# A four-layer graph network on one core: layer 0's edge loop with the expanded rows added on TensorE, the next expansion ahead of the sums, and the weights' store on ScalarE's queue

## What is computed

```python
xl = (x @ W_l + b_l).reshape(n, HEADS, C)
xr = (x @ W_r + b_r).reshape(n, HEADS, C)
e = (edge_attr @ W_e).reshape(-1, HEADS, C)
g = leaky_relu(xl[src] + xr[dst] + e, NEG_SLOPE)
logits = einsum('ehc,hc->eh', g, att)
ex = exp(logits - amax[dst])            # amax: segment_max over dst
msg = xl[src] * (ex / (denom[dst] + 1e-16))[..., None]
out = segment_sum(msg, dst)
...
def mlp2(x, w1, b1, w2, b2):            # layer 1's per-edge weights, wk and wv
    return relu(x @ w1 + b1) @ w2 + b2
```

## Time and profile before

| | us |
|---|---|
| median of 3 runs (lowest, highest) | 7575.63 (7556.03, 7577.67) |
| the profiled execution | 7521.62 |
| its span, first to last instruction | 7519.8 |

### The profile page before, as it was taken

How to read it: one execution, slowest core, us unless ns; L and a number is a source line. 1 busy time by engine, 2 the same in 40 slices (tenths; PEclk the granted TensorE clock), 3 DMA queues, 4 the chain that set the end, 5 groups by cost and what they waited for, 6 DMA issues and landing times. The chain is left out here.

```text
span 7519.8 us, 68661 instructions
## 1 busy us (share of the span) xinstructions
PE 3287.9 (44%) x16209; PEld 2672.0 (36%) x16209; DVE 4250.7 (57%) x6312; ACT 2199.0 (29%) x3619; POOL 3742.6 (50%) x3396
## 2 busy tenths in 40 slices
PE   0677777447666676666676666300000034000000
PEld 0444444246666666666666666300000033000000
DVE  2677777546666666666666666545555543222223
ACT  0555555313222232222222222122222213111111
POOL 4666666543233333333333333277777722767674
PEclk8787888778888888888888888655555558555555
DMA  7666666422222222222222222133333316212111
GB/s 236 199 223 211 215 218 211 140 74 78 75 78 76 73 79 75 79 76 74 78 75 78 76 77 75 53 85 94 95 94 97 95 44 284 50 46 52 46 48 40
DMA packets 396267, 784.61 MB, mean 104 GB/s; under 512 B 169068, under 2 KB 192368, under 8 KB 367684
## 3 DMA queue, kind: packets, MB, share of 16 engines
q1 hardware_dynamic: 227540, 499.20, 20.0%
q0 software_dynamic: 112240, 142.03, 8.5%
q10 hardware_dynamic: 56448, 142.93, 5.0%
HBM read 392.79 MB, written 390.85 MB: 104 GB/s over the span
## 5 line engine op out<-in xcount | busy, mean ns | idle before, releaser
L1194 POOL DMA_INDIRECT G<-x_tab,IDX_src x784 | 1009.8, 1288 | 2108.2 <-DMA IDX_src<-src 1852.9
L1231 PE MATMUL COLS<-CF,XF 128*128 128x256 f32 x4704 | 1220.9, 398 | 0.0
L697 POOL DMA_INDIRECT G<-xl_tab,IDX_src x784 | 852.4, 1087 | 392.3 <-issue 253.3
L1310 DVE TENSOR_TENSOR XS<-G,S 128x2560 f32<-128x2560 f32 x196 | 553.0, 2822 | 871.6 <-DMA G<-x_tab,IDX_src 867.7
L1236 PE MATMUL COLS<-CHI,XHI 128*128 128x256 f32 x1568 | 610.8, 390 | 972.1 <-DVE XHI L1323 971.4
L1468 PE MATMUL CP<-IDENT,LROW 128*68 128x128 f32 (+1 forms) x15 | 4.3, 422 | 2309.9 <-DVE SM L1544 2309.9
L697 POOL DMA_INDIRECT G<-kv_tab,IDX_src x784 | 846.1, 1079 | 269.2 <-issue 259.4
L697 POOL DMA_INDIRECT G<-rel_tab,IDX_rel x784 | 767.9, 979 | 324.1 <-issue 248.1
L1231 PEld LDWEIGHTS COLS<-CF,XF 128*128 128x128 f32 x4704 | 892.9, 204 | 98.3
L1277 ACT ACTIVATE XF<-RING 128x512 f32<-128x512 f32 x588 | 330.0, 595 | 1686.9 <-PE RING L1216 1656.6
L1468 PEld LDWEIGHTS CP<-IDENT,LROW 128*68 128x68 f32 (+1 forms) x15 | 1.9, 157 | 2311.6 <-DVE SM L1544 2311.5
(11 more groups left out here) (232 smaller groups left out, 6123.6 us busy)
## 6 DMA issues: line engine op xcount, KB each, us to landing
wkv_tab<-WKV SPq DMA_DIRECT2D x98, 1024.0 KB
WKV<-wkv_tab SPq DMA_DIRECT2D x98, 1024.0 KB, 5.0
scan<-OUT ACTq DMA_DIRECT2D x196, 288.0 KB
scan<-OUT ACTq DMA_DIRECT2D x98, 576.0 KB
rel_tab<-YS SPq DMA_DIRECT2D x25, 2048.0 KB, 7.1
RAW<-spread SPq DMA_DIRECT2D x196, 256.0 KB
spread_q<-ZQ SPq DMA_DIRECT2D x98, 512.0 KB
Q<-spread_q SPq DMA_DIRECT2D x98, 512.0 KB, 3.6
```

What stands on the lines that cost most here:

```text
L697: pool.indirect_dma_start(out=self.G[g][b][:, c, :], out_offset=None, in_=tab, in_offset=bass.IndirectOffsetOnAxis(ap=self.IDX[which][b][: ...
L1194: pool.indirect_dma_start(out=e.G[0][b][:, col, :], out_offset=None, in_=x1_tab, in_offset=bass.IndirectOffsetOnAxis(ap=e.IDX["src"][b][:, ...
L1231: nc.tensor.matmul(acc, XF[h][:, k, edges_], CF[:, k, :], start=(k == 0), stop=False)
L1310: nc.vector.tensor_tensor(XS[:, j, :, :], e.G[0][b][:, j, :].unsqueeze(2).to_broadcast([P, 4, SH + 1, 64]), S9[b][:, j, :].unsqueeze(3).to ...
```

## The change

The attributes come transposed from the host (input `ea16t`), so the transpose, its PSUM bank TR and ACT's copy go. PROJ and ATTR_T become pairs. The product of the attributes (`attributes`) is issued for chunk t+1 after `weigh` of t and leaves the bank open; a second product with the identity adds the expanded rows XE to the same bank, once they are there, and closes it. DVE's add of XE goes, and its add of PROJ now reads G and PROJ. DVE expands chunk t+1 between the logits and the sums of t. ACT's `turn` runs two chunks ahead. The store of WKV is issued by ACT behind the four copies, with a wait for them, and not by SP two chunks later.

```diff
@@ SP
-                        def store_weights(t, n, b):
-                            wait(sp, wkv_out, t * 4 + 4)
-                            sp.dma_start(row_view(wkv_tab, t), WKV[b][:, :, :]).then_inc(wkv_stored[b], 16)
-
...
                             if not first:
-                                wait(sp, attr_t, t - 1)
-                            sp.dma_start(ATTR[b][:, :, :], row_view(ea16, t)).then_inc(e.attr_in[b], 16)
+                                wait(sp, projected, t - 1)
+                            sp.dma_start(ATTR_T[b][:, :], ea16t[bass.ds(t, 1), :, :].rearrange("a p n -> p (a n)"))\
+                              .then_inc(e.attr_in[b], 16)
...
-                            if not isinstance(t, int) or t >= 2:
-                                store_weights(t - 2, n - 1, b)
@@ PE
+                        def attributes(t, n, b, early):
+                            wait(pe, e.attr_in[b], (n + 1) * 16)
+                            if not early:
+                                wait(pe, proj_used, t - 1)
+                            nc.tensor.matmul(PROJ[b][:, :], ATTR_T[b][:, :], WE8[:, :, :].rearrange("p j f -> p (j f)"),
+                                             start=True, stop=False)
...
-                            nc.tensor.transpose(TR[:, 0:P], ATTR[b][:, :, :].rearrange("p j f -> p (j f)"),
-                                                IDENT[:, :]).then_inc(attr_t, 1)
                             if first:
+                                attributes(0, 0, 0, True)
                                 hide(0, 0, 0, True)
-                            wait(pe, attr_c, t + 1)
-                            if not first:
-                                wait(pe, proj_used, t)
-                            nc.tensor.matmul(PROJ[:, :], ATTR_T[:, :],
-                                             WE8[:, :, :].rearrange("p j f -> p (j f)"), start=True, stop=True)\
-                              .then_inc(projected, 1)
+                            wait(pe, e.expanded, t + 1)
+                            nc.tensor.matmul(PROJ[b][:, :], IDENT[:, :],
+                                             e.XE[b][:, :, 1:1 + C].rearrange("p f j -> p j f"),
+                                             start=False, stop=True).then_inc(projected, 1)
                             if not last:
                                 hide(t + 1, n + b, 1 - b, False)
                             weigh(t, n, b, first)
+                            if not last:
+                                attributes(t + 1, n + b, 1 - b, first)
@@ ACT
-                        def ahead(t, n, b, first):
-                            e.turn(act, t, n, b, first)
-                            wait(act, attr_t, t + 1)
-                            if not first:
-                                wait(act, projected, t)
-                            nc.scalar.activation(ATTR_T[:, :], TR[:, 0:P], ACT.Copy).then_inc(attr_c, 1)
...
+                            wait(act, wkv_out, t * 4 + 4)
+                            act.dma_start(row_view(wkv_tab, t), WKV[b][:, :, :]).then_inc(wkv_stored[b], 16)
...
                             e.factors(act, t, n, b, first)
+                            if not isinstance(t, int) or t < NCH - 2:
+                                e.turn(act, t + 2, n + 1, b, False)
                             if not last:
-                                ahead(t + 1, n + b, 1 - b, False)
                                 rectify(t + 1, 1 - b, isinstance(t, int) and t < 1)
@@ DVE
-                            st.then(nc.vector.tensor_tensor(T[:, :, :], e.G[0][b][:, :, :],
-                                                            e.XE[b][:, :, 1:1 + C].rearrange("p f j -> p j f"),
-                                                            ALU.add))
                             wait(v, projected, t + 1)
-                            nc.vector.tensor_tensor(T[:, :, :], T[:, :, :],
-                                                    PROJ[:, :].rearrange("p (j f) -> p j f", j=C),
+                            nc.vector.tensor_tensor(T[:, :, :], e.G[0][b][:, :, :],
+                                                    PROJ[b][:, :].rearrange("p (j f) -> p j f", j=C),
                                                     ALU.add).then_inc(proj_used, 1)
...
-                            e.expand(v, t, n, b, first)
+                            if first:
+                                e.expand(v, 0, 0, 0, True)
                             logits(t, n, b, first)
+                            if not last:
+                                e.expand(v, t + 1, n + b, 1 - b, False)
                             e.sums(v, t, n, b, first, e.G[0][b][:, :, :])
```

More of the change, by code:

```diff
@@ L53, with graph_kernel @@
 V_ALL = 64 * len(V_NAMES)
[L56 removed]
+def graph_kernel(nc, x, dst_shifted, src, ea16t, ea64t, ea9, etype, ew, w64, we, cfix, w2, b1, b2, wout, vecs, basis,
                  out):
@@ L829, in edges_0 @@
                 e = Edges(ctx, 0, [(xl_tab, 64, "src")], {"src": src_ap})
-                ATTR = e.pair("ATTR", [P, C, 16])
-                ATTR_T = sb("ATTR_T", [P, P], F32, ctx)
+                ATTR_T = e.pair("ATTR_T", [P, P])
                 WE8 = sb("WE8", [P, C, 64], F32, ctx)
@@ L839, in edges_0 @@
                 B2R, ONER = sb("B2R", [P, 2, 256], F32R, ctx), sb("ONER", [P, P], F32R, ctx)
-                TR, PROJ = e.bank("TR"), e.bank("PROJ")
+                PROJ = [e.bank("PROJ0"), e.bank("PROJ1")]
                 HID = [e.bank("HID0"), e.bank("HID1")]
                 WK = [e.bank(f"WK{i}") for i in range(4)]
-                attr_t, attr_c, projected, we_in, cleared = (e.sem("attr_t"), e.sem("attr_c"), e.sem("projected"),
-                                                             e.sem("we_in"), e.sem("cleared"))
+                projected, we_in, cleared = e.sem("projected"), e.sem("we_in"), e.sem("cleared")
                 proj_used = e.sem("proj_used")
@@ L886, in step @@
                             sp.dma_start(row_view(spread_q, t), ZQ[:, :, :]).then_inc(spread_q_zeroed, 16)
-                            if not isinstance(t, int) or t >= 2:
-                                store_weights(t - 2, n - 1, b)
                         chunks(sp, step)
-                        for b in range(2):
-                            store_weights(NCH - 2 + b, NCH // 2 - 1, b)
-                        for b in range(2):
-                            wait(sp, wkv_stored[b], NCH // 2 * 16)
                         wait(sp, spread_q_zeroed, NCH * 16)
@@ L993, in _ @@
                         e.drain_stores(act)
+                        for b in range(2):
+                            wait(act, wkv_stored[b], NCH // 2 * 16)
                     @block.vector
@@ L1713 @@
         "src": padded(a["src"].astype(np.int32), EPAD).reshape(P, J),
-        "ea16": padded(a["edge_attr_16"], EPAD),
+        "ea16t": padded(a["edge_attr_16"], EPAD).reshape(P, NCH, P).transpose(1, 2, 0),
         "ea64t": padded(a["edge_attr_64"], EPAD).reshape(P, NCH, C // 2, 2, 64).transpose(1, 3, 4, 2, 0)
```

10 lines of the change are left out of this document (4 added, 6 removed).

## The result

The changed kernel is slower: 7692.3 us (median of four, 7680.6 to 7701.6) against 7576.7 for the kernel before on the same chip (7556.0 to 7581.2). The ratio is 1.0157, 95% interval 1.0133 to 1.0181. The forecast was 7481 and a range that ended at 7568.

What follows compares the result with a forecast made beforehand. The prediction took POOL's gathers to bound layer 0's chunk after the change: 11.3 plus 0.35 of remaining waits, 11.65 for 12.63; 97 chunks by 0.98 save 95 us, giving 7481 us, range 7433 to 7568.

Steps and rivals of the forecast that it cites:

- What is late next: Layer 0's chunk after the change: DVE some 8.5 us, PE's circle on average 10.7, POOL 11.4 and so the bound.
- I can't name that disturbance; I carry it as a size: PE's late end after weighing a chunk (L928): some 3.5 us in one chunk, about 2 on average, added to PE's circle.
- POOL's floor: POOL's gathers and issue in layer 0's loop, work it can't drop: 11.3 to 11.4 us a chunk.
- The prediction's own sign of being wrong: DVE's add waiting over 1 us for PROJ would show that PE's circle binds.
- the rival of POOL's full floor and of shorter gathers: POOL reaches 11.3 us a chunk or its gathers shorten too: gain 129 us or more, 7446 to 7430; chance 0.15.
- Part 1 and 2: Transpose (0.27 us) and ATTR_T copy (0.28) go, with ACT's 3.3 us wait; DVE's first add goes, 1.08 a chunk.
- Part 3: PE's added identity product: 1.3 us a pair taken, from 1.12 to 2.0, or 3.7 at the low clock.
- Part 4: DVE's early expansion fills its 1.2 us wait before MSG, delays MSG by 0.5; its 0.9 wait for PROJ mostly goes.
- Part 5: ACT's turn two chunks ahead, needing the RAW load earlier: no cost taken, bound 0 to 0.5 us of wait.
- Part 6: Weights' store issued by ACT: SP loses its wait, POOL its 0.80 us index wait; ACT gains a 0.63 us issue.
- The slow rival: ACT's register instructions become 0.7 us each, seven a chunk: 0.8 a chunk too long, 75 us slower, 7650; chance 0.09.
- nothing is gained: the disturbance grows with PE's load and takes up all: PE's late ends in layer 0's loop use up the gain: 12.6 us a chunk, 7576; chance 0.08.

Runs made afterwards that it cites:

- a_short_pause: The changed kernel with a 128x256 memset on POOL, waited for, ahead of each chunk's gathers: 7506.5 us, 0.9917 of the kernel before.
- a_ease0: The changed kernel with POOL waiting, ahead of a chunk's gathers, until PE has finished the previous chunk's PROJ product: 7510.7 us, 0.9923 of the kernel before.
- a_ease_third: a_ease0 once more, on another chip with the kernel before at 7575.3: 7510.7 us, 0.9914 of the kernel before.
- b_act_store: The kernel before with the weights' store moved to ACT and nothing else: 7512.2 us, 0.9998 of the kernel before.
- b_third: The kernel before without an edit, on a chip where it takes 7311.0: 7316.8 us (one run).
- a_third: The changed kernel without an edit, on the chip with the kernel before at 7311.0: 7238.1 us, 0.9897 of the kernel before.
- a_fmajor_ease: a_ease_third with PROJ laid out feature by feature, so the identity product reads runs of 8 floats: 7501.0 us, 0.9902 of the kernel before.
- a_late_tiny: The changed kernel with the expansion back behind the sums and a waited-for 128x16 memset on POOL before each chunk's gathers: 7338.9 us, 1.0036 of the kernel before.
- a_tiny_pause: The changed kernel with a waited-for 128x16 memset on POOL ahead of each chunk's gathers: 7325.2 us, 1.0015 of the kernel before.
- a_fmajor_late: a_late_tiny with PROJ laid out feature by feature, so the identity product reads runs of 8 floats: 7278.2 us, 0.9954 of the kernel before.

## Why the prediction was wrong

1. **The step that failed** is in "What is late next": the late end of PE's L928, "I can't name that disturbance; I carry it as a size", 3.5 us or 2 on average. It was no size. It was the hold-up, inside a run of 16 gathers (798.38 to 820.73 in the stretch of the earlier trace rows), and with the change the waits that it causes went from 3 to 9 us each to 13 to 15, 28 times in the loop. PE's results then come only when POOL has run out of buffers, and POOL in turn waits for the DVE that waits for PE. In the terms of the sum: POOL's floor came as forecast, (473.0+159.5) us of gathers and issue in 400 to 1200 us, at 14.43 a chunk 11.4 each; the wait that was to stay, 0.35, is 171.7 us for the buffer, 3.1 a chunk. That is the loss. The prediction's own sign of being wrong came with it: the add waits over 1 us for PROJ, 207.5 us or 3.7 a chunk. What is shown: a_short_pause, a_ease0 and a_ease_third have the whole change and a break or a wait on POOL, and their ratios are 0.9914 to 0.9923. What isn't: that POOL's lost waits are the reason by themselves. b_act_store lost the index wait and makes the long runs, and loses no time; which part of the change has to join them was not isolated.
2. The sum, 12.63 to 11.65, came out as 11.68 to 10.88 where nothing is held up (chunk times of b_third and a_third): 0.80 a chunk against 0.98, 73 us against 95. POOL's waits fell to nothing, not to 0.35, and its floor is itself lower, 10.9 where the sum had 11.3, with gathers of 1.05 us against 1.12 in b_third: the rival of POOL's full floor and of shorter gathers (0.15) is what this chip shows. The gain is still smaller because the kernel before was already 0.95 faster there. On the chips with hold-ups the change with a break gains 61 to 65 us.
3. Part 1 and 2 held. The DVE add is 687 ns and the one of 1079 is gone; ACT's 209.3 us before ATTR_T are gone, and what is late in their place is EX for ARG, as said.
4. Part 3, the identity product, was mis-sized: taken 1.3, measured 1.98 for the pair at 811.90 and in the mean of a_third (146.9 us by 74), with a contiguous pair beside it at 1.02. That is the upper end. The nearest row by access pattern (ACT's strided copy, a factor of 1.8) was the better guide than the nearest by engine. The Trainium skill's note on "cachelines" (SBUF — State Buffer) says that an access that crosses to a new line of 16 bytes pays a penalty. At the full clock the trace agrees for PE: 1096 ns read float by float in a_ease_third, 611 in runs of 8 floats in a_fmajor_ease, though that run crosses lines too. The "3.7 at the low clock" is wrong, though. At a granted clock of 0.50 the strided pair takes 2.17, hardly more than at 1.00 (2.06), and a contiguous one 2.08, so there the step costs next to nothing. Two pairs of a_late_tiny, the first at 0.50 and the second at 1.00:

```profile
459.79 2.17 PE L940 MATMUL PROJ<-XE,IDENT 128*128 128x512 f32 x2 [3.20 <-DVE XE L685]
471.67 2.06 PE L940 MATMUL PROJ<-XE,IDENT 128*128 128x512 f32 x2 [1.45 <-DVE XE L685]
```

   In the changed kernel the step costs nothing to tell (8.2 us of waiting in a_third), since the early expansion covers it; without that cover it costs 0.58 a chunk.
5. Part 4, the early expansion, is that cover. Its price by itself, a_late_tiny against a_tiny_pause, is 0.09 us a chunk, over two chips and so only roughly.
6. Part 5 held with the store moved: ACT waits 4.9 us for RAW over 74 chunks (a_third). Without it, 5.6 a chunk.
7. Part 6: the index wait went (2.1 us in a_third), the store on ACT costs nothing, and its move by itself brings nothing either (0.9998), though the prediction had counted POOL's 0.80 us of index wait as time to win. The slow rival's mechanism, slow register instructions on ACT, didn't come: L819's MOVE on ACT takes 29 ns at the median and 38 at most in the profile after. They showed on SP, in the profile before too, and they didn't decide what the change cost: a_short_pause has 147 of them and gains.
8. The rival "nothing is gained: the disturbance grows with PE's load and takes up all" had the right object. That PE's load drives it isn't shown; it goes away with a break in POOL's issuing, and nothing caps it at the gain.

Rows of before told of it, and I passed over them. These stand beside the earlier trace rows, and the prediction used their numbers:

```profile
812.25 1.26 ACT L970 ACTIVATE HT<-HID,B 128x512 f32<-128x512 f32 x2
814.59 0.69 DVE L1015 TENSOR_TENSOR T<-T,PROJ 128x512 f32<-128x512 f32 x1 [2.21 <-PE PROJ L944]
821.06 1.43 DVE L760 TENSOR_TENSOR_SCAN SC<-DEC,MSG 128x612 f32<-128x612 f32 x1
```

PE's late end (ACT goes on at 812.08), its effect on the add, and SP's issues of 0.68 to 0.69 us at 803.35 and 820.65 all lie in that one run of POOL. Two engines slow at once, with no wait that explains either, asked for a look at what they have in common and at what changes the size. (SP's slowness turned out to stay where PE's long late ends go, so one cause for both isn't shown.)

What stays open: why a run of gathers delays what PE does, why on some chips only, and why the delay passes by itself in the kernel before and in b_act_store and not after the change. The kernel with long runs and all of the change but one part was never run on a chip with hold-ups, except for the expansion, and that one broke the runs as well; the identity product was left out only where nothing is held up. In the changed kernel even a run of 8 and one of 9 gathers have such a wait (12.7 and 4.6 us). The records don't say whether PE's products run late or only their signals arrive late, since PE's ends are modelled. That the break's length doesn't matter beyond some point is seen only from 1.1 us upward on a chip with hold-ups; shorter ones (16 elements) ran only where there are none. And the rest of the program, with nothing changed in it, takes 6282 to 6301 us on the chips with hold-ups and 6175 to 6189 on the others, so something slows more there than this loop.

## To carry to other kernels

A wait that looks like the thing to remove can be what keeps other engines on time: before removing POOL's idle time, look at who comes free when POOL stops. An end that comes late for no reason in the trace is a cause not yet found, and must not enter a sum as a constant; line it up against what every engine was doing, queues included. When a long run of indirect DMAs is made longer, try one short break in each chunk beside it, and measure on more than one chip.

## What the hardware showed

- While POOL issues gathers 0.30 us apart, on some chips the engines that read PE's results wait for them without a releaser in the trace, 28 times 12.7 to 14.7 us in the changed kernel and at most 9.0 in the kernel before; a break of 1.1 us after every 8 gathers all but removes it (34 waits over 3 us to 3, and 1.0153 to 0.9917). On two other chips runs of 112 gathers do no harm.
- On the same chips SP's register instructions in the loop take up to 1.4 us where they take at most 0.051 on the others, with the break or without it (147 of 1162 and 241 of 1167 over 0.3 us).
- Chips, or sets of runs, differ by 3.5% on the kernel before (7311 to 7577 us). Of the 205 to 213 us between the profiled spans (7519.8 against 7315.0 and 7307.0) 92 to 96 lie in this loop and the rest outside it. A change's sign can differ with them: 1.0157 and 0.9897.
- A 128x512 product with a moving operand read float by float at a step of nine takes 1.07 to 1.16 us at the full clock, where one in runs of 8 floats takes 0.61 in the mean and a contiguous one 0.59. At half the clock a pair of them takes 2.17 us strided and 2.08 contiguous, so the step costs time at the full clock alone.
- DVE's add of two 128x512 operands takes 0.69 us with the PSUM operand contiguous or read with a step of eight floats (a_third, a_fmajor_late), and 1.08 with an SBUF operand read at a step of nine (L1011 in the earlier trace rows).
